# Half of the low probability parts, the key projection and the denominators moved between engines in a Macaron block (Trainium2, one core)

## What is computed

```
x = x + 0.5 * ffn(layernorm(x), w_up, w_down)
x = x + attention(layernorm(x), Wq, Wk, Wv, Wo)
x = x + 0.5 * ffn(layernorm(x), w_up, w_down)
```

```
g = einsum('bld,lg->bgd', x, one_hot)                       # sums over 16 tokens
side_k = einsum('bgd,dhk->bghk', g, Wk)                     # side_v likewise
logits = einsum('bnqhd,bnkhd->bnhqk', qb, k_cat) + bias     # 3*128 local + 128 side keys
m = max(x.max(axis), 0);  unnorm = exp(x - m)
probs = unnorm / (unnorm.sum(axis) + exp(-m))               # one extra logit of zero
y = einsum('bnhqk,bnkhd->bnqhd', probs, v_cat);  out = einsum('blhk,hkd->bld', y, Wo)
```

## Time and profile before

| | us |
|---|---|
| median of 3 runs | 2192.09 (2191.43 to 2194.49) |
| the profiled execution, its own time | 2187.97 |
| its span, first to last instruction | 2186.2 |
| first turned DMA of the attention phase issued / last | 332.5 / 1923.6 |
| PE busy | 2061.4 (94%) |
| ACT busy | 1932.2 (88%) |
| DVE busy | 1886.4 (86%) |
| POOL busy | 1322.1 (60%) |

### The profile page before, as it was taken

The page is one execution under the profiler, slowest core; times in us unless marked ns, Lnnn a source line. Parts: engine busy times, 40 slices in busy tenths (PEclk is TensorE's granted clock), DMA queues, the critical chain, the costliest instruction groups (busy, mean ns, idle before and its releaser), DMA issues. The chain is left out here.

```text
span 2186.2 us, 77384 instructions
## 1 busy us (share of the span) xinstructions
PE 2061.4 (94%) x30283; PEld 1595.0 (73%) x30283; DVE 1886.4 (86%) x4775; ACT 1932.2 (88%) x4178; POOL 1322.1 (60%) x1295
## 2 busy tenths in 40 slices
PE   4999988999999999999999999999999999979999
PEld 2677767777777777777777777777777777756666
DVE  6999967999899898999888999898888999867776
ACT  4899848999999899999989999999999999969997
POOL 2223315777777677777767777776777777722221
PEclk9999989999999999999999999999999999999999
DMA  6888737999999999999999999999999999958898
GB/s 193 154 163 161 150 68 110 168 176 173 169 173 172 136 172 172 170 170 170 176 146 158 172 171 177 173 171 157 148 171 174 175 171 176 163 91 175 180 179 181
DMA packets 1341580, 355.53 MB, mean 163 GB/s; under 512 B 1321760, under 2 KB 1340192, under 8 KB 1341216
## 3 DMA queue, kind: packets, MB, share of 16 engines
q1 hardware_dynamic: 1341216, 350.59, 100.0%
HBM read 14.68 MB, written 8.39 MB: 11 GB/s over the span
## 5 line engine op out<-in xcount | busy, mean ns | idle before, releaser
L985 POOL TENSOR_TENSOR probs_split<-probs,probs_split 128x512 f16<-128x512 f32 (+1 forms) x1026 | 1149.0, 1133 | 421.0 <-DVE probs_split L1327 297.6
L1315 DVE CUSTOM_DVE_ANT_0 probs<-score_ps,mask,neg_qk_scale 128x512 f32<-128x512 f32 (+1 forms) x1028 | 740.9, 721 | 90.0 <-PE score_ps L1086 88.4
L1247 ACT ACTIVATE probs<-probs,minus_max 128x512 f32<-128x512 f32 (+1 forms) x1027 | 718.6, 700 | 92.6 <-DVE minus_max L1315 86.9
L1108 PEld LDWEIGHTS y_ps<-v_parts,probsT 128*128 128x128 f16 x11904 | 467.0, 98 | 74.6 <-DMA probsT<-probs_split 3.5
L1108 PE MATMUL y_ps<-v_parts,probsT 128*128 128x64 f16 x11904 | 513.7, 193 | 4.0 <-DMA probsT<-probs_split 3.9
L1263 ACT ACTIVATE probs_split<-probs 128x512 f16<-128x512 f32 (+1 forms) x770 | 471.1, 612 | 17.3 <-DMA probsT<-probs_split 3.0
L1083 PE MATMUL score_ps<-k_parts,q_parts 64*128 64x384 f16 (+3 forms) x2604 | 379.9, 286 | 20.7 <-DVE minus_max L1315 17.5
L1086 PE MATMUL score_ps<-k_parts,q_parts 64*128 64x384 f16 (+3 forms) x2604 | 379.9, 286 | 0.0
L1083 PEld LDWEIGHTS score_ps<-k_parts,q_parts 64*128 64x128 f16 x2604 | 195.6, 94 | 138.2 <-DVE minus_max L1315 45.3
L1015 PE MATMUL item_ps<-b_xT,wk_split 128*128 128x128 f16 x3168 | 220.4, 219 | 39.7 <-DVE b_xT L1307 36.1
L1015 PEld LDWEIGHTS item_ps<-b_xT,wk_split 128*128 128x128 f16 x3168 | 180.6, 98 | 62.8 <-DVE b_xT L1307 41.7
(11 more groups left out here) (165 smaller groups left out, 3633.1 us busy)
## 6 DMA issues: line engine op xcount, KB each, us to landing
probsT<-probs_split SPq DMA_TRANSPOSE x1025, 3.9
out_x<-x_resident SPq DMA_DIRECT2D x64, 128.0 KB, 2.0
x_resident<-in_L_attn_x SPq DMA_DIRECT2D x56, 128.0 KB, 2.7
h_a<-in_L_ffn_w_up SPq DMA_DIRECT2D x1, 1024.0 KB, 5.8
scratch_a<-in_L_ffn_w_down SPq DMA_DIRECT2D x1, 1024.0 KB, 8.1
x_resident<-in_L_attn_x SPq DMA_DIRECT2D x2, 512.0 KB, 9.4
raw_q_a<-in_L_attn_Wq SPq DMA_DIRECT2D x1, 1024.0 KB, 11.8
raw_k_a<-in_L_attn_Wk SPq DMA_DIRECT2D x1, 1024.0 KB, 11.8
```

The lines of the kernel that those rows point to most:

```text
L985: nc.gpsimd.tensor_tensor(parts_of[ring(at, v)][:, LO, low_columns(place_of(at, v))], probs[v % NBUF][:, cols], parts_of[ring(at, v)][:, H ...
L1108: last = nc.tensor.matmul(out, pt[ring(at, v)][:, low * a + t, :], vr[:, slot, b, h * DH:(h + 1) * DH], start=(n == 0), stop=(n == len(pas ...
L1247: nc.scalar.activation(probs[v % NBUF][:, cols], probs[v % NBUF][:, cols], ACT.Exp, bias=bias[:, j % 2, h:h + 1], scale=-1.0, accum_out=su ...
L1315: nc.vector.tensor_tensor_reduce(out=probs[v % NBUF][:, cols], in0=score_ps[v % NBUF][:, cols], in1=mask_of(at, v), scale=w.neg_qk_scale[: ...
```

## The change

- **Items.** K0 and K1 go two slots later in each block, and OUTP is cut in two: its first two pieces (which need only the first half of y) stand in slots 6 and 7, ahead of K0, its last two in slots 10 and 11, between K0 and K1. The two PSUM banks for items are now given by a table (`BANK_OF`).
- **Low halves.** In every fourth unit DVE makes the low half too, by a subtraction right behind its cast (it waits for the cast). POOL makes the low halves of the other three only. `plo_done` becomes four semaphores.
- **Denominators.** The sum of 8 columns moves from DVE (slots 1 and 9) to POOL (slots 6 and 14, behind its low half). DVE's reciprocal stays in slots 2 and 10.
- **Side sums.** In the first phase the second normalised x is split in float16 halves, the high one by ACT (`second_high`), the low one by POOL (`second_low`); PE sums both with float16 products: 16-bit ones, twice as many. The squares become bfloat16, to make room.
- **Start.** The sum over partitions at L266 is made by a turn on PE, a sum on DVE and a small product on PE.

```diff
-    V1, Q0, XTR, Q1, K0, YT1, K1, OUTP, YT0, V0 = PLAIN = range(10)
+    V1, Q0, XTR, Q1, YT1, K0, OUTP, K1, YT0, V0 = PLAIN = range(10)
...
-    PIECES = [[(V1, 0)], [(V1, 1)], [(Q0, 0)], [(Q0, 1)], [(XTR, 0), (Q1, 0)], [(Q1, 1)], [(K0, 0)], [(K0, 1), (YT1, 0)],
-              [(K1, 0)], [(K1, 1)], [(OUTP, 0)], [(OUTP, 1)], [(OUTP, 2)], [(OUTP, 3)],
+    PIECES = [[(V1, 0)], [(V1, 1)], [(Q0, 0)], [(Q0, 1)], [(XTR, 0), (Q1, 0)], [(Q1, 1)], [(OUTP, 0)], [(OUTP, 1), (YT1, 0)],
+              [(K0, 0)], [(K0, 1)], [(OUTP, 2)], [(OUTP, 3)], [(K1, 0)], [(K1, 1)],
...
             def split_low(at, v):
 
+                if v % 4 == CAST_BY_DVE:
+                    return
...
+            def denominators(at, v):
+                j, h = divmod(v, H)
+                eight = slice(h - 7, h + 1)
+                extra_done.wait(pool, at.halves + 2 * j + half(v))
+                nc.gpsimd.tensor_tensor(denom[:], sums[:, j % 2, eight], extra[:, j % 2, eight],
+                                        ALU.add).then_inc(denom_done.sem, 1)
...
                     split_low(at, u + SPLIT_AHEAD)
+                    if h in (6, 14):
+                        denominators(at, u + 1)
...
                 nc.vector.tensor_copy(parts_of[ring(at, v)][:, HI, cols], probs[v % NBUF][:, cols]
                                       ).then_inc(phi_done[v % 4], 1)
+                dve.wait_ge(phi_done[v % 4], at.quarters + v // 4 + 1)
+                nc.vector.tensor_tensor(parts_of[ring(at, v)][:, LO, low_columns(place_of(at, v))], probs[v % NBUF][:, cols],
+                                        parts_of[ring(at, v)][:, HI, cols], ALU.subtract).then_inc(plo_done[v % 4], 1)
...
-                    if h in (1, 9):
-                        denominators(at, u - 2)
...
+            def second_low(p):
+                pool.wait_ge(xn2hi_ready, p + 1)
+                nc.gpsimd.tensor_tensor(xn2_parts[LO][p % 2], xn2[p % 2], xn2_parts[HI][p % 2],
+                                        ALU.subtract).then_inc(xn2lo_ready, 1)
...
+            def second_high(p):
+                act.wait_ge(xn2_ready, 2 * p + 2)
+                if p >= 2:
+                    act.wait_ge(side_done, p - 1)
+                nc.scalar.activation(xn2_parts[HI][p % 2], xn2[p % 2], ACT.Copy).then_inc(xn2hi_ready, 1)
...
-                        last = nc.tensor.matmul(g_ps[:, k, c * GPB:(c + 1) * GPB], xn2[half][:, c % 2, k * P:(k + 1) * P],
-                                                group32[:], start=True, stop=True)
+                        for s in (HI, LO):
+                            last = nc.tensor.matmul(g_ps[:, k, c * GPB:(c + 1) * GPB],
+                                                    xn2_parts[s][half][:, c % 2, k * P:(k + 1) * P], w.group16[:],
+                                                    start=(s == HI), stop=(s == LO))
...
-                pool.wait_ge(absum_ready, 2)
-                nc.gpsimd.partition_all_reduce(absum_all[:], absum[:], P, RADD).then_inc(absum_everywhere, 1)
...
+                pe.wait_ge(absum_ready, 2)
+                nc.tensor.transpose(g_bank[0:2, 0:P], absum[:], w.ident32[:]).then_inc(absum_turned, 1)
+                pe.wait_ge(absum_summed, 1)
+                nc.tensor.matmul(g_bank[:, P:P + 2], ones4[0:2, :], diagonal2[:], start=True,
+                                 stop=True).then_inc(absum_everywhere, 1)
```

More of the change, by code:

```diff
@@ L662, in _ @@
                     x_hi(2 * (t + 1) + i - 2)
+                if first and i in (1, 2) and 2 <= t < NTILE + 2:
+                    second_high(2 * (t - 2) + i - 1)
                 if chunk_of(n):
@@ L837, in place @@
                 at = len(prefix) + self.offset(j, kind)
-                banked = [n for n in range(at) if order[n] not in TURNS]
-                before = sum(n >= len(prefix) for n in banked) if j >= 0 else -1
-                return bank_of_item(len([k for k in PRE_ORDER if k not in TURNS]) + before), at - banked[-2]
+                same = [n for n in range(at) if order[n] not in TURNS and BANK_OF[order[n]] == BANK_OF[kind]]
+                return item_ps[BANK_OF[kind]], at - same[-1] if same else None
         class End(At):
```

83 lines of the change are left out of this document (45 added, 38 removed).

## The result

| | before | changed |
|---|---|---|
| median, us | 2191.76 (2190.98 to 2194.49, 4 runs) | 2360.7 (2358.74 to 2362.09, 4 runs) |
| the profiled execution's span | 2186.2 | 2360.4 |
| first row maximum of attention | 326.5 | 320.9 |
| last row maximum of attention | 1923.1 | 2094.6 |
| first up product of the third phase | 1942.2 | 2114.0 |

The changed kernel is slower: the ratio is 1.0775, with a 95% interval from 1.0761 to 1.0788. The forecast was 2363.0 with a range from 2330 to 2420.

The account below looks back on a forecast made before the run. A chain changing sides between ACT and DVE was taken to set the pace. From 2187.97: +161 inner blocks, +12 edge blocks, 0 side sums, +2 phase's end, -4 start gave 2359; 4.1 to the median gave 2363 us, range 2330 to 2420.

Parts of the forecast that it names:

- The chain: Attention's inner blocks: ACT and DVE wait for each other in turn; each subtraction adds 0.73 us, four times; chance 0.76.
- stretches: Four-unit parts of an inner block, cut at row maxima of slots 1, 5, 9, 13; together 27.56 us against 24.69.
- The rival in which the waits absorb it: Attention: DVE's idle time takes up the subtractions, about 2151 us, ACT's wait staying at 0.3 us; chance 0.07.
- Edge blocks: Attention's 8 blocks with 384 columns and more PE work: 1.5 us more each, 12 us, bounds 0 and 2.87 each.
- First phase and start: Ahead of attention: side sums 0 (from -10 to +10), phase's end about +2, start without the reduction -4 us.
- Denominators: Attention: taking these 0.66 us sums off DVE gains 0, since DVE then waits for an item's high part.
- D: Inner block's fourth stretch, from slot 13's row maximum to the next block's slot 1: 6.15 us, forecast 7.20.
- Half of OUTP ahead of K0: Attention: removes PE's 37.1 us wait for the new xT; at most 11 us alone, 0 in the new chain.
- B: Inner block's second stretch, between the row maxima of slots 5 and 9: 6.90 us, forecast 6.86.
- C: Inner block's third stretch, between the row maxima of slots 9 and 13: 5.41 us, forecast 6.54.
- POOL's hold: Attention: POOL's work delays DVE's subtraction by up to 1.14 us; once a block 64 us more, 2427; chance 0.10.
- A: Inner block's first stretch, between the row maxima of slots 1 and 5: 6.23 us, forecast 6.96.

Follow-up runs that it names:

- e1: Changed kernel with the low halves of all units made by POOL again, DVE keeping the cast alone: 2188.19 us.
- e2: Kernel before, with only DVE's low half behind its cast in every fourth unit added: 2366.01 us.
- e11: Changed kernel with DVE making the low half in every eighth unit instead of every fourth, POOL the rest: 2270.42 us.
- e8: Kernel before with the changed feed-forward phases only, its attention as it was: 2186.74 us.
- e7: Kernel before with DVE's cast moved behind the row maximum of the same slot: 2192.73 us.
- e12: Changed kernel with denominators back on DVE, plus an unused sum of 8 columns on POOL in slot 14: 2363.98 us.
- e3: Kernel before with the changed order of items and its banks alone: 2195.44 us.
- e4: Changed kernel with the denominators back on DVE in slots 1 and 9: 2391.69 us.
- e5: Changed kernel with DVE's subtraction made twice, first into a spare tile that nobody reads: 2661.46 us.
- e9: Changed kernel with all low halves on POOL and DVE's cast behind the row maximum of its slot: 2188.49 us.
- e6: Changed kernel with the subtraction behind the row maximum of the same slot instead of ahead of it: 2294.17 us.
- e13: Changed kernel, all low halves on POOL, cast behind the maximum, two further 256-byte DMAs a block on SP: 2228.23 us.

## Why the prediction was right, step by step

**The total: closer than its parts.** The forecast's sum came out within 2.3 us partly by luck. Attention lost 4 us more than its terms, the first phase gained 3.6 more, the way behind attention and the third phase cost 2.7 that had no term; and the 4.1 us that the forecast put between the profiled execution and the median came out as -1.4 (2362.09 and 2360.7).

**The chain.** The predicted stretches 6.96, 6.86, 6.54 and 7.20 came out as 6.95, 6.86, 6.51 and 7.20, the block as 27.52 instead of 27.56. The step that carries it, 0.45 to the subtraction and 0.61 behind it for the 0.33 that were there, is what the rows show, and e1, e2 and e11 show that each of the four places pays it in full. The rival in which the waits absorb it falls by its own sign: ACT's wait is 1.0 to 1.1 us, not 0.3. 56 inner blocks give 56 x 2.82 = 158, for the 161 of the sum.

**Edge blocks: mis-sized.** I took 1.5 us each, half of an inner block's. At a border between two sequences, three blocks in a row take 82.4 us after (27.03, 27.76, 27.66) and 74.6 to 75.3 before: 2.4 to 2.6 each. So attention lost 177 in place of 173. With 384 columns there are as many casts and subtractions in the chain.

**First phase and start: somewhat low.** The forecast had -4 for the start, 0 for the side sums and +2 at the end; measured are -4.7 to the first up product (32.8, now 28.1), -2.0 from there to the last one, +1.1 behind: -5.6. PE fell from 100.00 to 91.14 of 100 us while DVE stayed full at 98.61, which fits that so little of PE's gain shows. e8 has the same 5 to 6 us in the time.

**Third phase: not foreseen.** It took 2.4 us more. PE's granted clock in its first 100 us is 0.97, in the same stretch of before 0.99:

```profile
2115.00:2215.00 100.00, 97.30 (x651) 65.02 (x650) 73.22 (x172) 89.70 (x119) 23.33 (x33) 0.97 0.83 161
```

The other profiles show that it is not the changed code. The third phase takes 244.0 to 244.5 us in nine of the fourteen profiles, with a granted clock of 0.98 to 0.99 in its first 100 us, and 246.1 to 246.3 in the other five, with 0.96 to 0.97. e7, whose third phase is that of the kernel before, is among the five (246.2); e8, with the changed one, is not (244.3). Each kernel was profiled once, so whether the same kernel shows both values is open.

**Denominators: right sum, wrong reason to call it safe.** In slots 1 and 9 they turn into waiting, as said. But the prediction held `b_x_normed` for something that could only get longer (0.95, by up to 0.5). It got shorter, 0.32, because it comes to POOL at a moment that lets it in: with the moved sum in the changed kernel (e12), and without it in e3. In D that changes nothing, since D is a loop over ACT by then with room enough for it: with 1.24 instead of 0.32 it costs 0.54 (e4), so some 0.4 of the 0.9 are cover. The 28 us that the range held ready for this were the right size.

**Half of OUTP ahead of K0.** 0 was right for the changed kernel. The bound of 11 us for it alone was too kind (and its 6.72 is 6.74, by the terms given): e3 shows nothing gained, since B's 0.78 comes back in C and D. The wait at K0's own new place (77.2 us in all) is one that the prediction had dismissed, since K0 is done two slots ahead; it costs nothing, as the stretches show, but it is there.

**POOL's hold.** It did not occur, and the margin was named rightly: 0.35 us in B (POOL's next low half starts at 598.91, DVE's subtraction at 598.56), 0.40 foreseen in A and 0.48 there (592.18 and 591.70). What did occur is the reverse: POOL's low half takes 1.36 and 1.23 us there instead of 1.16. e5 shows what some 0.6 us more would have cost: 0.97 each time.

## What to carry to other kernels

Cut the repeating stretch at one kind of instruction, and find the loop in which each of two engines waits for the other; what is put between the release of one and the release of the other is paid in full, each time, with all engines less busy than before. Work that costs nothing by sums belongs behind the instruction that the other engine waits for, not ahead of it, and then one has to look at what it meets there: here POOL's hold took more than half of it back. Ahead of removing one limit, price the next ones: taking 0.33 us off the chain in four places of a block gained nothing (e7, e9), since the next limit, SP's issues at some 24.5 us, was only 0.2 below the block's 24.7.

## What the runs showed of the hardware

An instruction on DVE with two inputs in SBUF, `b_x_normed` or the cast with one in float32, and one of POOL's low halves do not share: whoever comes second waits until the first has ended. DVE's second subtraction in e5 took 1.57 us from start to start instead of 0.60. The rest are durations of one instruction: the denominators 0.66 in the mean before, 0.46 in e4 and 0.18 in e7, `b_x_normed` 1.31 in e4, 1.24 in e7 and 0.40 in the changed kernel; POOL's sum of 8 columns 0.65 instead of 0.20 (e6), and its low halves 1.36 instead of 1.16 when DVE was first. The Trainium skill, "SBUF — State Buffer", section "SBUF: two separate sides", calls the shared pair of ports an exclusive lock that whichever starts first keeps for the whole instruction; the traces agree, with these numbers. Low parts of items, which read one input from PSUM (0.69), show no such wait next to the same POOL instructions. Casts seldom meet one: in 51 blocks of the kernel before the low half ends some 0.13 us into a cast, which takes its 0.42 all the same; in four it ends 0.28 us into it, and there the cast takes 0.56 and ends 0.28 us behind POOL's end (1104.99):

```profile
1103.82 1.17 POOL L985 TENSOR_TENSOR probs_split<-probs,probs_split 128x512 f16<-128x512 f32 x1 [0.21 <-ACT probs_split L1263]
```
```profile
1104.71 0.56 DVE L1327 CAST probs_split<-probs 128x512 f16<-128x512 f32 x1
```

What I had not expected is how narrow the moment is between two of POOL's instructions that stand back to back: DVE got in between them when its instruction started 0.21 us ahead of the first one's end (e3), and had to wait for the second one too when it started 0.06 or less ahead (e4, and four blocks of e3).

A turned DMA takes SP 1.29 us in the median, but 1.53 in the mean from one to the next (e9, 58.28 us for 38); a plain one of 256 bytes 0.42 (e13). TensorE's granted clock was 0.93 in the mean in e5, with PE busy for 81.34 us of 100 and waits of up to 2 us ahead of its scores, and 1.00 in the changed kernel at 86.38. In e5 the blocks with the lower clock at the start of A are the shorter ones (31.85 against 32.81): it made PE late just enough to get DVE's subtraction past POOL.
